# Two banks for the running tile products, and batch 1's normalised rows made by VectorE instead of TensorE transposes

## The chip, the cores and the metric

One Trainium2 chip, one of its cores. The time is the device time of one launch in microseconds. Before the change it is 2794.61 us, the median of three runs (2794.59 to 2795.62). The profiled execution, from which every row below comes, took 2796.74 us, with a span of 2794.9 us from its first to its last instruction and a mean granted TensorE clock of 0.997.

## The reference, cut to what matters

One transformer block with adaptive modulation, on x of shape (2, 2048, 576), with 16 heads of 36 and a hidden width of 2304.

```python
mod = swish(c) @ w_mod + b_mod
sh_msa, sc_msa, g_msa, sh_mlp, sc_mlp, g_mlp = split(mod, 6, axis=1)
xn = _ln(x) * (1 + sc_msa[:, None, :]) + sh_msa[:, None, :]
qkv = xn @ w_qkv + b_qkv
q, k, v = heads of qkv
q = _ln(q, g_q);  k = _ln(k, g_k)
attn = softmax(q k^T * HD ** -0.5)
x = x + g_msa * ((attn v) @ w_proj + b_proj)
xn2 = _ln(x) * (1 + sc_mlp) + sh_mlp
x = x + g_mlp * (gelu(xn2 @ w1 + b1) @ w2 + b2)
```

`_ln` subtracts the mean over the last axis and divides by the root of the variance plus 1e-6, on the 576 features of a row for xn and on the 36 features of a head for q and k.

## The kernel before, in words

Nearly full precision is had from 16-bit matmuls: each factor is cut into a high and a low f16 half, and three products are added. A tile of 128 rows times the 432 columns of one group of heads (q, k and v of four heads) takes 14 matmuls (`split_products`, which `tile_products` issues).

**Order of the work.** After a start (modulation, batch 0's rows normalised, turned and multiplied for the first group of heads) come 8 groups G, one for each batch and four heads: 0 to 3 are batch 0, 4 to 7 are batch 1. A group is 16 units u, a unit is one head and 512 queries, and a unit has 8 steps s. In a step

- TensorE makes two score matmuls (`scores`) and, three steps behind (LAG), four matmuls of probabilities with v (`sums`);
- ScalarE takes the exponential of 128x1024 scores into `p` (line 697);
- VectorE takes the low part `plo` of it (line 890), which `sums` needs.

`scores` of a step needs the exponential of two steps before; the exponential of a step needs `sums` of four steps before; both are semaphore counts with credits given at the start. Every engine executes its own list of instructions in order, and waits where that list says so.

**The tile that runs along.** In each unit one tile of the next group is made. TensorE issues seven of its matmuls in step 0 and seven in step 1, all into one PSUM bank (`tile_bank`), after a wait until VectorE has read the tile before out of it (`t_yn`). ScalarE copies v out in step 2 and squares q and k in step 3, VectorE sums the squares in step 3 (`tile_sum`), GpSimd adds eps and takes the power -0.5 (lines 568 and 570), VectorE scales in step 6 (`tile_normal`, lines 854 and 857), and in the next unit ScalarE writes the high parts in steps 0 and 1 (`tile_high`, `tile_high_again`) and VectorE the low parts in step 1 (`tile_low`, line 863). SyncE then issues one DMA transpose into `qkT` of the next group; the first scores of that group wait for the last of them.

**Batch 1's rows.** They are made beside batch 0's attention. In group 0 VectorE takes their statistics. In group 1 (`Y_IN`) VectorE normalises one tile of 128 rows in each unit (lines 914 and 917) and SyncE stores it to `y_dram`. In group 2 (`HATS_IN`) SyncE loads it back, TensorE turns it with five f32 transposes into `hat_bank` (`hat_turns`, line 1139), ScalarE applies scale and shift while it reads the bank (`hats`, line 669) and makes the high half, and VectorE makes the low half (lines 921 and 922). `tile_products` reads them from group 3's last unit on.

**Weights.** In units 1 to 8 of groups 0 and 1 the weights of the third and fourth heads' groups are centred and cut (`sum_word`, `centre_word`, `high_word`, `low_word`). In groups 4 to 6 ScalarE and VectorE cut one slice of the later weights per unit in step 5 (`word_high`, `word_lower`, lines 679 and 868).

**GpSimd** makes the v operands of the next head once in four units (`head`, lines 549 to 553), in units 2, 6, 10 and 14, after that unit's power.

**Group 7** makes no tiles; instead the projection and the first part of the MLP of the first 512 rows begin there (`rest.tensor_early`, `vector_early`, `gpsimd_early`): GpSimd adds two partial sums in units 1, 3, 4, 5 and 7 (line 1511), VectorE multiplies by the inverse denominators in step 3 of the same units, which it had inverted in step 5 of group 6's last unit (line 1597). After group 7 the MLP is TensorE work almost alone.

Of the kernel before, what the change touches and what calls it, by code (L numbers as in the profile page):

```python
# [17 lines left out]
HD = H // NH  # L18
# [41 lines left out]
class Start:  # L60
# [9 lines left out]
    def __init__(self, nc, ctx, keep, place, ps, wq, xhi, x, c, w_mod, b_mod, w_qkv, b_qkv, g_q, g_k, b2, gates_dram):  # L70
# [20 lines left out]
        later = [sb(f"later{g}", [P, QK, N // 2], F32, at) for g, at in ((2, 126720), (3, 75520))]  # L91
# [10 lines left out]
        self.gates_ready, self.gates_stored = sem("gates_ready"), sem("gates_stored")  # L102
        self.landed = [sem(f"landed{g}") for g in range(self.AHEAD)]
# [193 lines left out]
    def centre_word(self, pool, n, i):  # L297
        m, heads = n * self.SLICED + i, self.word[n][i][:, 0:2 * GW].rearrange("p (e d) -> p e d", d=HD)
        pool.wait_ge(self.w_sum, m + 1)
        pool.tensor_scalar(self.lone_mean[:, :], self.lone[:, :], 1.0 / HD, None, ALU.mult).then_inc(self.w_mean, 1)  # L300
# [42 lines left out]
def attention_mlp(nc, keep, place, x, c, w_mod, b_mod, w_qkv, b_qkv, g_q, g_k, b2, sums_dram, den_dram, rden_dram, y_dram, out, halves,  # L343
# [3 lines left out]
    with ExitStack() as ctx:  # L347
# [4 lines left out]
        STATS_IN, Y_IN, HATS_IN = NG - 4, NG - 3, NG - 2  # L352
        PARTS = ((0, 0, 4, 2, 0), (1, 0, 4, 4, 1), (2, 0, 2, 5, 2), (2, 2, 4, 6, 3), (3, 0, 2, 7, 4), (3, 2, 3, 8, 5), (3, 3, 4, 9, 5))
        RAWS, STORED = 9, (4, 4, 2, 2, 2, 2)
# [36 lines left out]
        hat_bank = ps[:, 6, :]  # L391
        tile_bank, second_bank = ps[:, 7, :], ps[:, 5, :]
# [13 lines left out]
        n_loaded, n_stats, n_mv, n_var, n_rstd, n_y, n_whole, n_stored = (  # L406
            sem("n_" + n) for n in ("loaded", "stats", "mv", "var", "rstd", "y", "whole", "stored"))
# [8 lines left out]
        ny_loaded, n_turned, n_aff, n_hi, n_lo = (sem("n_" + n) for n in ("y_loaded", "turned", "aff", "hi", "lo"))  # L416
# [3 lines left out]
        ends = Ends(t_mm, t_yn, t_stored, scores_ready, head_ready, pv_done, exp_done, oT_ready, oT_stored, n_lo)  # L420
        start = Start(nc, ctx, keep, place, ps, wq, xhi, x, c, w_mod, b_mod, w_qkv, b_qkv, g_q, g_k, b2, gates_dram)
        rest = Mlp(nc, ctx, keep, place, ps, ends, x, sums_dram, den_dram, rden_dram, out, halves, b1, gates_dram)
        block = ctx.enter_context(nc.Block())

        @block.sync
        def _(sp):
# [23 lines left out]
            start.load_tail(sp)  # L450
            start.load_b2(sp, y_ready)
            sp.wait_ge(start.rows_ready, 2)
            turn_heads(0)
# [7 lines left out]
            start.load_words(sp, 0)  # L461
# [15 lines left out]

            def unit(G, u):
# [3 lines left out]
                if G == Y_IN:  # L482
                    if u == 0:
                        sp.wait_ge(n_mv, NT + 1)
                    sp.wait_ge(n_stored, 16 * u + 16)
                    sp.dma_start(xy[:, 0:H], xf[bass.ds(N + u * P, P), :]).then_inc(n_loaded, 16)
                if G == HATS_IN:
                    if u == 0:
                        sp.wait_ge(n_stored, 16 * NT + 16)
                    sp.wait_ge(n_lo, u + 1)  # L490
                    sp.dma_start(xy[:, :], y_dram[bass.ds(u * P, P), :]).then_inc(ny_loaded, 16)
# [12 lines left out]
                if G < GROUPS - 1:  # L504
                    sp.wait_ge(t_low, U + 2)
                    sp.wait_ge(t_high, 2 * U + 3)
                    sp.dma_start_transpose(qkT[(G + 1) % 2][:, :, bass.ds(u * P, P)],
# [31 lines left out]
        def _(pool):  # L539
# [73 lines left out]
            for m in range(1, 5):  # L613
                power(m)
# [1272 lines left out]
```

## Time and profile before

| | us |
|---|---|
| median of the runs | 2794.61 |
| the profiled execution | 2796.74 |
| its span | 2794.9 |
| TensorE busy | 2750.6 |
| VectorE busy | 1988.5 |
| ScalarE busy | 1517.0 |
| GpSimd busy | 669.4 |

Shares of busy time say little here, because three parts follow on each other: the start, to 103.5 us; the eight groups, to 1821.8 us; and the rest. Within the groups the exponential (line 697) that opens each unit is a good clock: from one to the next is a unit.

### The profile page before, as it was taken

Reading aid. Unit: us, or ns where it says so; the run is one execution under the profiler, and the core shown is the slowest. Engines: PE = TensorE matmul, PEld = TensorE weight load, DVE = VectorE, ACT = ScalarE, POOL = GpSimd, SP = SyncE. Lnnn points to the kernel's source line nnn. Section 1 sums busy time; section 2 is a strip of 40 time slices with the busy share of each in tenths; the row PEclk is TensorE's granted clock in tenths of the full one; section 3 lists DMA queues with packets and bytes.
Section 4 is the critical chain, followed back from the end, with each engine's and each line's share of the span. In section 5 each row is a group of like instructions: output and inputs, shape, how many; then the busy total and the mean of one; then the engine's idle time right before and its main releaser. Section 6 shows DMA issues by size and latency. Waiting matters only on the chain.

```text
span 2794.9 us, 42813 instructions
## 1 busy us (share of the span) xinstructions
PE 2750.6 (98%) x14754; PEld 1415.5 (51%) x14754; DVE 1988.5 (71%) x2699; ACT 1517.0 (54%) x2232; POOL 669.4 (24%) x526
## 2 busy tenths in 40 slices
PE   6999999999999999999999999999999999999999
PEld 3444444444444444444444434447566575756656
DVE  7799999888888888888898899953534334353421
ACT  4777777788877777777777777621111112111110
POOL 2553343323233333333343321200000000000000
PEclk9999999999999999999999999999999999999999
DMA  6512322222211122223223243041120202112000
GB/s 222 96 32 66 92 75 79 76 52 48 53 30 32 34 66 67 69 68 74 70 75 78 53 119 112 14 156 53 40 76 16 91 13 79 51 41 76 16 18 18
DMA packets 238609, 181.28 MB, mean 65 GB/s; under 512 B 151511, under 2 KB 187805, under 8 KB 237765
## 3 DMA queue, kind: packets, MB, share of 16 engines
q1 hardware_dynamic: 238182, 179.31, 23.5%
q8 instruction: 96, 1.57, 0.2%
q14 instruction: 43, 0.35, 0.0%
q10 hardware_dynamic: 288, 0.04, 0.0%
HBM read 99.70 MB, written 46.04 MB: 52 GB/s over the span
## 4 chain that ended last, share of the span: by engine, by line
PE 93%; DVE 3%; ACT 1%; issue 1%; SPq 1%; DMA 1%; POOL 1%; ACTq 0%; DVEq 0%
PE at_ps L1760 19%; PE at_ps L1109 15%; PE at_ps L1106 15%; PE at_ps L1097 15%; PE at_ps L1786 15%; PE at_ps L1128 10%; DVE at_plo L890 2%; PE at_ps L1161 1%; PE at_ps L1779 1%; PE at_ps L1724 1%; PE at_ps L1741 1%; ACT at_p L697 0%; DMA st_wm_first<-in_L_cond_b_mod 0%; PE at_ps L210 0%; PE at_ps L1139 0%
## 5 line engine op out<-in xcount | busy, mean ns | idle before, releaser
L890 DVE TENSOR_TENSOR at_plo<-at_p 128x1024 fp32r<-128x1024 f32 x1024 | 1267.9, 1259 | 184.5 <-ACT at_p L697 181.7
L697 ACT ACTIVATE at_p<-at_ps 128x1024 f32<-128x1024 f32 x1024 | 1047.5, 1026 | 407.2 <-PE at_ps L1097 406.4
L1109 PE MATMUL at_ps<-at_plo,at_vr 128*37 128x512 f32 x2048 | 1073.5, 592 | 0.0
L1106 PE MATMUL at_ps<-at_p,at_v 128*73 128x512 bf16 x2048 | 797.2, 389 | 4.9 <-DVE at_plo L890 4.7
L1760 PE MATMUL at_ps<-ml_w2s,ml_hid 128*128 128x288 f16 x3456 | 429.8, 287 | 2.0 <-issue 2.0
L1760 PEld LDWEIGHTS at_ps<-ml_w2s,ml_hid 128*128 128x128 f16 x3456 | 338.7, 98 | 87.9 <-issue 2.5
L1786 PE MATMUL at_ps<-ml_xhi,ml_w 128*128 128x512 f16 x1296 | 381.9, 379 | 0.0
L1106 PEld LDWEIGHTS at_ps<-at_p,at_v 128*73 128x73 f16 x2048 | 232.8, 114 | 249.6 <-DVE at_plo L890 10.5
L568 POOL TENSOR_TENSOR at_tssq<-at_tssq,head_eps 128x8 f32<-128x8 f32 x112 | 123.8, 1106 | 959.8 <-DVE at_tssq L850 959.8
L1109 PEld LDWEIGHTS at_ps<-at_plo,at_vr 128*37 128x37 f32 x2048 | 233.7, 114 | 221.7 <-issue 0.7
L1097 PE MATMUL at_ps<-at_qk_even 109*128 (+1 forms) x1024 | 310.1, 385 | 2.4 <-ACT at_p L697 2.4
L1097 PE MATMUL at_ps<-at_qk_odd 109*128 (+1 forms) x1024 | 309.5, 384 | 0.0
L1128 PE MATMUL at_ps<-at_wq,at_xhi 128*128 128x432 f16 x1008 | 295.8, 348 | 4.3 <-DVE at_txc L854 3.7
L1642 DVE TENSOR_TENSOR ml_part<-at_ps,ml_gates 128x576 f32<-128x576 f32 x64 | 48.5, 757 | 348.1 <-PE at_ps L1760 348.1
L1568 ACT ACTIVATE ml_g<-at_ps,ml_b1col 128x512 f32<-128x512 f32 x144 | 96.2, 686 | 362.6 <-PE at_ps L1779 249.8
L570 POOL TENSOR_TENSOR at_tssq<-at_tssq,power 128x8 f32<-128x8 f32 x112 | 248.3, 2217 | 8.8
L1551 ACT ACTIVATE ml_aff<-at_ps,cols 128x512 f32<-128x512 f32 x40 | 31.0, 776 | 345.8 <-PE at_ps L1724 345.8
L1786 PE MATMUL at_ps<-ml_xlo,ml_w 128*128 128x512 f16 x576 | 218.3, 379 | 0.0
L1688 DVE CAST ml_hid<-ml_g 128x512 f16<-128x512 f32 x144 | 61.2, 425 | 201.8 <-ACT ml_g L1568 201.8
L1786 PEld LDWEIGHTS at_ps<-ml_xhi,ml_w 128*128 128x128 f16 x1296 | 123.5, 98 | 157.6 <-issue 15.7
L1128 PE MATMUL at_ps<-at_wq,at_xlo 128*128 128x432 f16 (+1 forms) x560 | 193.9, 346 | 0.0
L1527 POOL TENSOR_TENSOR ml_rstd<-ml_mv,eps 128x4 f32<-128x4 f32 x7 | 1.4, 202 | 741.8 <-DVE ml_mv L1676 741.8
(182 smaller groups left out, 2280.3 us busy)
## 6 DMA issues: line engine op xcount, KB each, us to landing
head_sums<-at_oT SPq DMA_DIRECT2D x256, 72.0 KB
ml_held<-head_sums SPq DMA_DIRECT2D x64, 256.0 KB
at_xy<-in_L_cond_w SPq DMA_DIRECT2D x34, 288.0 KB
w_halves<-at_wq SPq DMA_DIRECT2D x68, 144.0 KB
at_xy<-in_x SPq DMA_DIRECT2D x32, 288.0 KB, 2.9
ml_x<-in_x SPq DMA_DIRECT2D x8, 1152.0 KB, 5.8
out<-ml_x SPq DMA_DIRECT2D x7, 1152.0 KB, 4.5
ml_held<-head_rden SPq DMA_DIRECT2D x24, 216.0 KB
```

Of the source, the lines that this page charges most:

```text
L568: pool.tensor_tensor(tssq[:, 1, :], tssq[:, 0, :], keep.head_eps[:, 0:QK], ALU.add).then_inc(t_msq, 1)
L570: pool.tensor_tensor(tssq[:, 1, :], tssq[:, 1, :], keep.power[:, 0:QK], ALU.pow).then_inc(t_rstd, 1)
L697: act.activation(p[:, s % NP, :], ps[:, 2 * (s % 2):2 * (s % 2) + 2, :].rearrange("p a n -> p (a n)"), ACT.Exp).then_inc(exp_done, 1)
L890: nc.vector.tensor_tensor(plo[:, s % NP, :], p[:, s % NP, :], high, ALU.subtract).then_inc(plo_ready, 1)
L1097: last = nc.tensor.matmul(ps[:, 2 * (s % 2) + a, :], qk[0:SW, GH + h, (2 * s + a) * P:(2 * s + a + 1) * P], qk[0:SW, h, bass.ds(qc * CH, C ...
L1106: nc.tensor.matmul(acc[0:VW, bass.ds((U % 2) * CH, CH)], v16[:, h % 2, 2 * s + a, 0:VW], high, start=(s == 0 and a == 0), stop=False, skip ...
L1109: last = nc.tensor.matmul(acc[0:RW, bass.ds((U % 2) * CH, CH)], vr[:, h % 2, 2 * s + a, 0:RW], plo[:, s % NP, a * CH:(a + 1) * CH], start= ...
L1128: last = nc.tensor.matmul(bank[:, 0:3 * GW], l, rhs[:, g * 3 * GW:(g + 1) * 3 * GW], start=(n == 0), stop=(n == len(ops) - 1))
L1568: act.activation(self.g32[:, f % 2, :], self.up_bank(f), ACT.Gelu_apprx_tanh, bias=self.b1col[:, f:f + 1], scale=1.0 / WS).then_inc(self.g ...
L1688: nc.vector.tensor_copy(self.hhi[:, f, :], self.g32[:, f % 2, :]).then_inc(self.hhi_ready, 1)
L1760: last = nc.tensor.matmul(self.pair(i)[:, half, :], l, w[:, half * HALF:(half + 1) * HALF], start=(n == 0), stop=(n == len(ops) - 1))
L1786: last = nc.tensor.matmul(self.up_bank(f), w, xs, start=first and n == 0, stop=not first and n == len(ops) - 1)
```

## The change

- **Two banks for tile products.** `tile_bank` becomes a function of the tile's number, banks 6 and 7 in turn. TensorE waits for the reading of the tile before last. VectorE's scaling of a tile (`tile_normal`) moves from step 6 to step 0 of the next unit, `tile_high` to step 1, `tile_high_again` and `tile_low` to step 2, the square and its sum to step 4. Unit 0 has the same order as the others.
- **eps by VectorE.** `tile_sum` is followed by a small VectorE addition; GpSimd's line 568 is gone, its power stays.
- **Batch 1's rows by VectorE.** Group 1's normalising and its store, group 2's load, TensorE's transposes and ScalarE's scaling are gone. In group 2, units 1 to 10, and group 3, units 1 to 6, one tile of 128 rows is handled per unit: SyncE loads x; VectorE in step 5 does `hat_scaled` and then `hat_shifted`, each 128x576; ScalarE in step 6 writes the high half in two copies (`hat_high`); VectorE in step 7 writes the low half (`hat_lower`, 128x576); SyncE issues two DMA transposes into `xhi` and `xlo`, and loads the next tile. Scale and shift are rows, stored to DRAM at the start (`store_mods`) and spread over the partitions by a load at the head of each of the two groups, where GpSimd adds 1 to the scale.
- **Start.** The last four tiles of the first 2048 rows are four parts of their own (before, two together and two alone); GpSimd's first half of `head_of` moves up between two powers; SyncE issues `load_words` behind the first unit's transpose, not ahead of it.
- **Group 7.** The inversion of the denominators moves from unit 15 to unit 14 of group 6, GpSimd's additions wait for the first `sums` of their own unit, and VectorE's multiplications move from step 3 to step 5.

```diff
-        PARTS = (..., (3, 0, 2, 7, 4), (3, 2, 3, 8, 5), (3, 3, 4, 9, 5))
-        RAWS, STORED = 9, (4, 4, 2, 2, 2, 2)
+        HATS = 10
+        SCALED_AT, SHIFTED_AT, HAT_HIGH_AT, HAT_LOW_AT = 5, 5, 6, 7
+        PARTS = (..., (3, 0, 1, 7, 4), (3, 1, 2, 8, 4), (3, 2, 3, 9, 5), (3, 3, 4, 10, 5))
+        RAWS, STORED = 10, (4, 4, 2, 2, 2, 2)
...
-        hat_bank = ps[:, 6, :]
-        tile_bank, second_bank = ps[:, 7, :], ps[:, 5, :]
+        tile_pair = ps[:, 6:8, :].rearrange("p a n -> p (a n)")
+        def tile_bank(X, c0, c1):
+            return tile_pair[:, bass.ds((X % 2) * CH + c0, c1 - c0)]
...
+            def load_hat(r):
+                sp.wait_ge(n_lo, r + 1)
+                sp.dma_start(xy[:, 0:H], xf[N + r * P:N + r * P + P, :]).then_inc(n_loaded, 16)
...
+                if U == 0:
+                    start.load_words(sp, 0)
...
+                if r is not None:
+                    sp.wait_ge(n_lo, r + 2)
+                    if hat_of(G, u + 1) is not None:
+                        load_hat(r + 1)
+                    for part, whole in ((hat_hi, xhi), (hat_lo, xlo)):
+                        sp.dma_start_transpose(whole[:, :, r * P:(r + 1) * P], part[G - HATS_IN]).then_inc(n_turned, 16)
...
             def tile_power(X):
-                pool.wait_ge(t_ssq, X + 1)
-                pool.tensor_tensor(tssq[:, 1, :], tssq[:, 0, :], keep.head_eps[:, 0:QK], ALU.add).then_inc(t_msq, 1)
                 pool.wait_ge(t_msq, X + 1)
...
+                if u == 0 and G in (HATS_IN, HATS_IN + 1):
+                    n = G - HATS_IN
+                    pool.wait_ge(n_rows, 16 * (n + 1))
+                    pool.tensor_scalar(scale_row[n], scale_row[n], 1.0, None, ALU.add)
+                    pool.memset(hat_lo[n][:, H:KC * P], 1.0).then_inc(n_hole, 1)
...
+            def hat_high(n, r):
+                act.wait_ge(n_hat, r + 1)
+                act.wait_ge(n_turned, 32 * r + 32)
+                act.copy(hat_hi[n][:, 0:H], xy[:, 0:H])
+                act.copy(hat_hi[n][:, H:KC * P], xy[:, KF * P:H]).then_inc(n_hi, 1)
...
-                    if tail and s == (1 if first else 0):
+                    if tail and s == 1:
                         tile_high(U)
-                    if tail and s == (2 if first else 1):
+                    if tail and s == 2:
                         tile_high_again()
...
-                    if fresh and s == 3:
-                        tile_square(X, second_bank if first else tile_bank)
-                    if G == HATS_IN and s == 5:
-                        hats(u, range(KF))
-                    if G == HATS_IN and s == 7:
-                        hats(u, (KF,))
-                        hats_high(u)
+                    if fresh and s == 4:
+                        tile_square(X)
+                    if hat is not None and s == HAT_HIGH_AT:
+                        hat_high(G - HATS_IN, hat)
...
             def tile_sum(X):
                 dve.wait_ge(t_sq, X + 1)
                 nc.vector.tensor_reduce(tssq[:, 0, :], txc[:, :, :], AX.X, ALU.add).then_inc(t_ssq, 1)
+                dve.wait_ge(t_ssq, X + 1)
+                nc.vector.tensor_scalar_add(tssq[:, 1, :], tssq[:, 0, :], HD * EPS * WS * WS).then_inc(t_msq, 1)
...
+            def hat_scaled(n, r):
+                dve.wait_ge(n_loaded, 16 * (NT + r + 1))
+                nc.vector.scalar_tensor_tensor(out=halved(xy[:, 0:H]), in0=halved(xy[:, 0:H]), scalar=nmv[:, r, 0:1], in1=scale_row[n],
+                                               op0=ALU.subtract, op1=ALU.mult).then_inc(n_scaled, 1)
+
+            def hat_shifted(n, r):
+                dve.wait_ge(n_scaled, r + 1)
+                nc.vector.scalar_tensor_tensor(out=halved(xy[:, 0:H]), in0=halved(xy[:, 0:H]), scalar=nrstd[:, 1, r:r + 1], in1=shift_row[n],
+                                               op0=ALU.mult, op1=ALU.add).then_inc(n_hat, 1)
+
+            def hat_lower(n, r):
+                dve.wait_ge(n_hi, r + 1)
+                nc.vector.tensor_tensor(hat_lo[n][:, 0:H], xy[:, 0:H], hat_hi[n][:, 0:H], ALU.subtract).then_inc(n_lo, 1)
...
-                    if tail and s == (2 if first else 1):
+                    if tail and s == 0:
+                        tile_normal(U)
+                    if tail and s == 2:
                         tile_low(U)
...
-                    if fresh and s == 3:
+                    if fresh and s == 4:
                         tile_sum(X)
-                    if fresh and s == 6:
-                        tile_normal(X, second_bank if first else tile_bank)
...
-                    if bank is tile_bank:
-                        pe.wait_ge(t_yn, X + 1)
+                    if not isinstance(X, int) or X >= 2:
+                        pe.wait_ge(t_yn, X)
...
-                    if G == HATS_IN and s == 4:
-                        hat_turns(u, range(KF))
-                    if G == HATS_IN and s == 7:
-                        hat_turns(u, (KF,))
...
+            pool.wait_ge(self.ends.pv_done, (self.UNITS_DONE - UNITS + u) * STEPS + 2)
...
-        if u in self.MULTIPLY_IN and s == 3:
+        if u in self.MULTIPLY_IN and s == 5:
```

## Rows read from the trace of the kernel before

**Rows 1.** Windows: groups 2, 3, 4 and 7, and what follows the groups

```profile
core 0: us, PE busy (x) PEld busy (x) DVE busy (x) ACT busy (x) POOL busy (x), PEclk, DMA share, GB/s
...
537.70:767.30 229.60, 226.87 (x1078) 107.17 (x1077) 192.86 (x243) 190.36 (x321) 58.43 (x52) 1.00 0.22 53
767.30:981.80 214.50, 214.50 (x990) 94.66 (x988) 181.03 (x209) 155.55 (x226) 76.51 (x52) 1.00 0.15 33
981.80:1197.20 215.40, 215.40 (x994) 94.97 (x993) 189.84 (x225) 163.33 (x240) 77.34 (x52) 1.00 0.26 66
1626.30:1821.80 195.50, 192.18 (x902) 85.99 (x900) 184.14 (x176) 143.13 (x154) 39.66 (x33) 1.00 0.29 89
1821.80:2794.90 973.10, 967.00 (x6407) 615.96 (x6404) 390.53 (x704) 163.57 (x251) 52.40 (x46) 1.00 0.16 52
```

**Rows 2.** Waits of TensorE in the groups, whole span: sum, times, longest

```profile
PE at_ps L1106 <- DVE at_plo L890: 4.7, 7, 1.2
PE at_ps L1128 <- DVE at_txc L854: 3.7, 9, 0.7
```

**Rows 3.** Groups of instructions, group 2: transposes, and the tile products' wait

```profile
L1128 PE MATMUL at_ps<-at_wq,at_xhi 128*128 128x432 f16 x146 | 42.8, 348 | 2.7 <-DVE at_txc L854 2.2
L1139 PE MATMUL at_ps<-ident,at_xy 128*128 128x128 f32 x80 | 13.9, 272 | 0.0
```

**Rows 4.** Timeline of ScalarE, one unit of group 3: start, duration, instruction

```profile
874.04 1.02 ACT L697 ACTIVATE at_p<-at_ps 128x1024 f32<-128x1024 f32 x1 [0.42 <-PE at_ps L1097]
874.96 0.43 ACT L643 CAST at_tstk<-at_txc 128x288 f16<-128x288 f32 x1
...
880.18 0.28 ACT L651 ACTIVATE at_v<-at_ps 128x144 f32 x1
880.40 0.58 ACT L663 COPY at_oT<-at_ps 73x512 f32 x1
880.88 1.02 ACT L697 ACTIVATE at_p<-at_ps 128x1024 f32<-128x1024 f32 x1
```

**Rows 5.** Timeline of VectorE, the same unit

```profile
881.93 1.23 DVE L890 TENSOR_TENSOR at_plo<-at_p 128x1024 fp32r<-128x1024 f32 x1 [0.39 <-ACT at_p L697]
883.07 0.45 DVE L850 TENSOR_REDUCE at_tssq<-at_txc 128x8 f32<-128x288 f32 x1
883.44 3.58 DVE L890 TENSOR_TENSOR at_plo<-at_p 128x1024 fp32r<-128x1024 f32 x3
887.32 0.46 DVE L854 SCALAR_TENSOR_TENSOR at_txc<-at_ps,at_tssq 128x288 f32<-128x288 f32 x1 [0.30 <-POOL at_tssq L570]
887.81 0.31 DVE L857 TENSOR_TENSOR at_txc<-at_txc,gain 128x144 f32<-128x144 f32 x1
888.04 2.35 DVE L890 TENSOR_TENSOR at_plo<-at_p 128x1024 fp32r<-128x1024 f32 x2
```

**Rows 6.** Timeline of TensorE: scores of step 1, one unit on

```profile
889.47 0.38 PE L1097 MATMUL at_ps<-at_qk_odd 109*128 x1
```

**Rows 7.** Groups of instructions, group 5: operations of 128x576, and the low parts

```profile
L868 DVE SCALAR_TENSOR_TENSOR at_wq<-at_xy,at_wq 128x576 f16<-128x576 f32 x16 | 12.0, 751 | 0.0
L679 ACT ACTIVATE at_wq<-at_xy 128x576 f16<-128x576 f32 x16 | 10.8, 675 | 0.0
L863 DVE TENSOR_TENSOR at_tstk<-at_txc,at_tstk 128x144 f16<-128x144 f32 x32 | 8.4, 304 | 0.0
```

**Rows 8.** Timeline of VectorE around a `head`, group 4

```profile
1023.01 5.00 DVE L890 TENSOR_TENSOR at_plo<-at_p 128x1024 fp32r<-128x1024 f32 x3
```

**Rows 9.** The same stretch on GpSimd: the longest operation of `head`

```profile
1024.70 2.24 POOL L553 TENSOR_TENSOR at_v<-at_v 128x576 f16<-128x576 f32 x1
```

**Rows 10.** Timeline of VectorE, end of group 6

```profile
1625.20 1.74 DVE L1597 RECIPROCAL ml_den<-ml_den 128x256 f32<-128x256 f32 x1
```

**Rows 11.** Timeline of TensorE: first unit

```profile
107.67 0.61 PE L1106 MATMUL at_ps<-at_p,at_v 128*73 128x512 bf16 x1 [1.18 <-DVE at_plo L890]
```

**Rows 12.** Transfers: issuer, number, median us from issue to landing

```profile
at_qk_even<-at_tstk SPq DMA_TRANSPOSE x48, 3.1
```

More of the change, by code:

```diff
@@ L132, in load_tail, with store_mods @@
         sp.dma_start(self.wm_tail[KT:KT + 1, :], self.b_mod[2 * H:6 * H].unsqueeze(0)).then_inc(self.wm_loaded[1][1], 16)
+    def store_mods(self, sp, mods_dram):
+        sp.wait_ge(self.rows_taken, 1)
+        for n, q in ((0, 32), (1, 0)):
+            sp.dma_start(mods_dram[n:n + 1, :], self.rows[0][q + 16:q + 17, 0:H]).then_inc(self.mods_stored, 16)
     def load_b2(self, sp, free):
@@ L405, in attention_mlp @@
             sem("t_" + n) for n in ("mm", "sq", "ssq", "msq", "rstd", "yn", "yg", "high", "low", "stored"))
-        n_loaded, n_stats, n_mv, n_var, n_rstd, n_y, n_whole, n_stored = (
-            sem("n_" + n) for n in ("loaded", "stats", "mv", "var", "rstd", "y", "whole", "stored"))
+        n_loaded, n_stats, n_mv, n_var, n_rstd = (sem("n_" + n) for n in ("loaded", "stats", "mv", "var", "rstd"))
+        n_rows, n_hole, n_scaled, n_hat, n_hi, n_lo, n_turned = (
+            sem("n_" + n) for n in ("rows", "hole", "scaled", "hat", "hi", "lo", "turned"))
         w_loaded, w_high, w_low, w_stored = sem("w_loaded"), sem("w_high"), sem("w_low"), sem("w_stored")
@@ L481, in unit @@
                     load_row(2 * u - UNITS)
[L482 to L491, printed above, removed]
+                r = hat_of(G, u)
+                if G in (HATS_IN, HATS_IN + 1) and u == 0:
+                    sp.wait_ge(scores_ready, G * UNITS * STEPS)
+                    both = start.later[G % 2][:, 2:6, HOLE // 2:HOLE // 2 + HALF]
+                    sp.dma_start(both, bcast(mods_dram.rearrange("v (a n) -> (v a) n", a=2), 0, P)).then_inc(n_rows, 16)
+                    load_hat(hat_of(G, 1))
                 i = U - SLICED * UNITS
@@ L612, in _ @@
                 pool.memset(stk[:, a, :, :, SW:P], 0.0).then_inc(start.stk_ready, 1)
-            for m in range(1, 5):
+            power(1)
+            head_of(0, 0, NT // 2)
+            for m in range(2, len(PARTS)):
                 power(m)
-            power(5)
-            power(6)
             tile_power(0)
-            head_of(0, 0, NT // 2)
             head_of(1, NT // 2, NT)
@@ L809, in _ @@
             square(4)
-            high(2)
             raw(7)
             square(5)
+            high(2)
             raw(8)
@@ L815, in _ @@
             high(3)
+            raw(9)
+            square(7)
             high(4)
+            high(5)
             tile_v(0, NT)
             tile_square(0)
-            high(5)
             high(6)
+            high(7)
             for G in range(GROUPS):
@@ L832, in _ @@
                     with act.Fori(start.SLICED + 2, UNITS - 1) as u:
+                        unit(G, u)
+                elif G in (HATS_IN, HATS_IN + 1):
+                    done, r0 = (HATS, 0) if G == HATS_IN else (NT - HATS, HATS)
+                    unit(G, 0)
+                    with act.Fori(1, done + 1) as u:
+                        unit(G, u, hat=u + r0 - 1)
+                    with act.Fori(done + 1, UNITS - 1) as u:
                         unit(G, u)
@@ L1084, in _ @@
                         unit(G, u, True)
-                    with dve.Fori(sliced, UNITS - 1) as u:
+                    for u in range(sliced, UNITS - 1):
                         unit(G, u)
@@ L1113, in sums, with tile_products @@
                 last.then_inc(pv_done, 1)
-            def tile_products(X, t, G, some, bank=tile_bank):
+            def tile_products(X, t, G, some):
                 ops = list(split_products(xhi, xlo, wq, bass.ds(t * P, P), slice(None)))
@@ L1218, in _ @@
             tile_products(0, 0, 1, range(0, 14))
[L1219 removed]
+            tile_products(1, 1, 1, range(0, 14))
             pe.wait_ge(start.gain_step, 4)
```

131 lines of the change are left out of this document (62 added, 69 removed).

## The prediction

> **What bounds the kernel now.** I read the windows first. In group 4 TensorE is busy for all of 215.4 us, in group 3 for all of 214.5 [rows 1]; a unit is 215.4 / 16 = 13.46 us and nothing but TensorE's own work sets it. VectorE is at 88% and ScalarE at 76% there, so both have room on average. Behind the groups TensorE is busy for 967.0 of 973.1 us, and the change leaves that part alone. Second, the waits: inside the groups TensorE waits 4.7 us for low parts of probabilities and 3.7 us for the bank of the tile products [rows 2]; that is all that better order can win, beside 2.4 us or so at the very start. Third, group 2, where batch 1's rows are turned: 229.6 us, 14.2 over group 4. Of this 2.7 us are waits, 2.2 of them for the bank, and the rest is TensorE's 80 transposes [rows 1, 3]. Last, the timelines of one plain unit on ScalarE, VectorE and TensorE [rows 4 to 6], because the question is whether the new work in 16 units still fits beside TensorE's 13.46 us.
>
> **What is removed.** Groups 2 and 3 together take 229.6 + 214.5 = 444.1 us. With neither transposes nor waits they are 32 units of 13.46, or 430.8: -13.3 us. The second bank also ends the waits for the bank outside group 2: 3.7 - 2.2 = 1.5 us [rows 2, 3], so -1.5; I see no bound of it but 0 and -1.5. Group 1's and group 2's row traffic through DRAM and VectorE's normalising in group 1 are hidden now and their removal gives nothing of its own. GpSimd loses the addition of eps; it has been idle most of the time, so that gives nothing either, and the small operation on VectorE costs some 0.1 us per unit under TensorE's work.
>
> **What is added, and whether it is hidden.** Three VectorE operations of 128x576 each: the one of that size that the trace has takes 0.751 us [rows 7], and the next VectorE instruction starts about 0.08 us ahead of a record's end (3.58 us for three low parts that start 1.14 apart [rows 5]). So 0.75 + 0.03 (the first waits for itself, as 854 and 857 show [rows 5]) + 0.67 + 0.67 = 2.1 us. A unit's VectorE work then is 8 low parts x 1.14 = 9.1, scaling 0.72 (887.32 to 888.04), tile low parts 0.44 (twice 0.22, their 0.304 less 0.08 [rows 7]), sum and eps 0.36 + 0.2, and 2.1: 13.0 us. That is under 13.46, so on the sum of work alone it fits. But these operations are strung on one chain with ScalarE's, and each engine is in order. I walk along it, with S the start of `hat_scaled` in step 5:
>
> - `hat_shifted` starts at S + 0.78 and its record ends at S + 1.53. VectorE goes on with the low part of step 6. ScalarE has been waiting at `hat_high` since it finished step 6's exponential. Its two copies take about 0.58 (0.675 less the overlap [rows 7]) and 0.12, so step 7's exponential starts at S + 2.3 and VectorE has it at S + 3.34 (a record of 1.02 and 0.04 until VectorE sees it).
> - VectorE: low part of step 7 to S + 4.48, `hat_lower` to 5.15, low part of step 0 to 6.29, then the tile's scaling, whose second operation is done at 7.12 (0.49 + 0.31 + 0.03 [rows 5]).
> - ScalarE waits for that in step 1 (`tile_high`), which takes 0.34 (0.43 less the overlap [rows 4]), so step 2's exponential starts at S + 7.46; its low part starts at 8.52.
> - ScalarE after it: 0.92 for the exponential (874.04 to 874.96), three copies of 144 columns of 0.2 each, 0.48 for the output copy (880.40 to 880.88) [rows 4]. Step 3's exponential starts at S + 9.5, its low part at 10.55.
> - VectorE: two low parts 2.28, sum and eps 0.58, low part of step 5 1.14. The next S is at S + 14.55.
>
> So the chain takes 14.5 us to come round, of which VectorE idles 1.5, against TensorE's 13.46: 1.1 us more per unit. TensorE does feel it. Its scores of step 1 need step 7's exponential, at S + 3.38. In the first such unit S is the low part of step 3, two more, the sum and eps, and one more: 881.93 + 1.14 + 1.14 + 0.58 + 1.14 = 885.93 on the plain unit's clock [rows 5], and the exponential is there at 889.31; the scores started at 889.47 [rows 6]. The first unit costs nothing and all slack is used up. Each later one adds 1.1: 9 x 1.1 - 0.1 = 9.8 in group 2 and 5 x 1.1 - 0.1 = 5.4 in group 3, together 15.2. What errs here is the sum of some fifteen durations; with 0.3 either way per unit (the low parts' gaps and the waits are what I know least) the 14 units give 11.0 to 19.4.
>
> On top comes `head` on GpSimd. When it runs, three low parts take 5.00 us where they take 3.58 otherwise, 1.4 us more [rows 5, 8]. In plain units TensorE covers that. In the new ones the chain is what counts; it has about 0.7 us of VectorE idle before step 7's low part and 0.4 twice later, so I take 0.9 of the 1.4. Units 2, 6, 10 of group 2 and 2, 6 of group 3 have a `head`, the one in unit 10 half outside: 4 x 0.9 = 3.6, bounds 0 and 5 x 1.4 = 7.
>
> The row of `head` shows it: its longest operation takes 2.24 us [rows 9] while the low parts beside it stretch by 1.4 in all. The Trainium skill, "SBUF — State Buffer", section "Who interferes with whom", says that a VectorE instruction with two SBUF inputs contends with a GpSimd instruction that reads SBUF, and that the one issued second blocks fully. All three new operations have two such inputs. The trace agrees in kind; by that rule each of them could lose a whole GpSimd operation, and what that would make is the second rival.
>
> New waits with no price as far as I see: the load of the next tile and the two DMA transposes are issued behind `hat_lower` (S + 5.2) and are wanted by S + 14.5 and S + 16.1; a transpose lands in 3.1 us [rows 12]. SyncE's queue has the unit's other transpose and the stores of sums between them, issued at about S + 10, and has room. At the end of a group the last tile's low part is now in step 2, at about 882.4 on the plain unit's clock, and with 3.1 us lands at 885.6, a good 1 us ahead of the next group's first scores, some 2.7 before 889.47 [rows 6, 12]. If it lands later, each of seven group boundaries pays.
>
> **Start and group 7.** In the first unit TensorE waits 1.18 us for the first low part [rows 11], which stood behind the tile's scaling on VectorE and now is ahead of it: -1.2, bounds 0 and -2.4. The start's four single tiles are more instructions for the same work, and GpSimd's powers are its chain; I count nothing. For group 7, 4.7 - 1.2 = 3.5 us of waits for low parts lie around it [rows 2, 11]. The inversion of 1.74 us [rows 10] stands between low parts where TensorE has no tile products to cover it; in unit 14 it has them, less the `head` there. GpSimd's second addition no longer follows directly on a `head`. The fifth unit's load of both a multiplication and a low part stays. I take half: -1.7, bounds 0 and -3.5.
>
> **The sum.** -13.3 - 1.5 + 15.2 + 3.6 - 1.2 - 1.7 = +1.1 us. The profiled execution took 2796.74, 2.1 more than the median of the runs, so this is 2797.8 for such an execution and 2795.7 for the median. A difference of 0.2%, 5.6 us, is about what can be told from none.
>
> **The rivals.** (1) *The chain does not bind.* VectorE's 13.0 us of work do fit, and if the exponentials catch up (ScalarE finds its operands ready, as it does in group 4) the new units stay at 13.46. Then 15.2 and 3.6 go: 2795.7 - 18.8 = 2777. For it speaks that group 1, with normalising on VectorE, runs without such a loss; against it, that group 1 had nothing for ScalarE to wait on between steps 6 and 7. A half-binding chain, 0.5 us a unit, gives 2777 + 7 + 1 = 2785. (2) *GpSimd's `head` blocks VectorE more than it did.* With more VectorE instructions of two inputs, each `head` costs its whole longest operation and more; at 2.24 each, five make 11.2 for my 3.6: 2795.7 + 7.6 = 2803, slower by 0.3%. It decides from 1.6 us a `head`, where the sum passes +5.6. For it speaks that the chain has no cover; against it, the rows of plain units, 1.4. (3) *A transpose lands late at the group boundaries*, in place of the wait for the bank: 7 x 1 us at most, 2802. (4) *The second bank gives nothing*, since VectorE's lateness only moves from the bank to the low parts: 1.5 less won, 2797, inside the first case.
>
> **How the numbers follow.** The forecast, a chain of 14.2 to 14.85 us, has 0.60, with its own range 2789 to 2802 (the 14 units' ends, and the other bounds taken half-way); of this 0.42 is within 0.2%, 0.08 faster, 0.10 slower. Rival 1 with its half-way case has 0.26, faster. Rivals 2 and 3 have 0.14, slower by over 0.2% nearly all. So faster 0.34, same 0.43, slower 0.23. The range has to take in rival 1's far end, 2777, with 2 us below it for its other terms' bounds (group 7 and the start could give 1.8 and 1.2 more), and go up to 2804.
>
> **What would show it.** Right: units of group 2 from the second to the tenth at 14.3 to 14.8 us and those behind them at 13.46; ScalarE's wait for `hat_shifted` of 2.5 us or so in each; TensorE's waits in these units at the scores, for exponentials, and hardly at the low parts; no wait of TensorE for the tile's scaling anywhere; no transposes by TensorE. Wrong: units at 13.5 there (rival 1), or TensorE waiting with low parts late after each `head` (rival 2), or scores waiting for a transfer in a group's first step (rival 3). The forecast fails first if one of the durations on the chain is not on it, for instance if the high copies start while the second operation still runs.

## The result and the profile after

The kernel after takes 2803.9 us, the median of eight runs (2801.55 to 2805.68); the kernel before takes 2795.1 beside it. The ratio is 1.0034, with a 95% interval of 1.0026 to 1.0043: slower by 0.3%. The forecast was 2795.7 and "no difference". The profiled execution took 2805.68 us with a span of 2803.6, 8.7 us over the span of before (2794.9). The forecast's range reached to 2804, which just takes the result in. That is luck: by the chain and its bounds alone it ended at 2802, and the rest was for costlier `head`s and late transfers.

The windows of the kernel after, group 2, 3, 4, 6, 7 and what follows:

```profile
core 0: us, PE busy (x) PEld busy (x) DVE busy (x) ACT busy (x) POOL busy (x), PEclk, DMA share, GB/s
532.82:764.81 231.99, 219.77 (x994) 94.00 (x992) 202.39 (x255) 157.46 (x244) 63.46 (x39) 1.00 0.27 58
764.81:990.39 225.58, 218.21 (x994) 94.44 (x993) 192.50 (x244) 155.68 (x237) 64.01 (x39) 1.00 0.24 50
990.39:1205.84 215.45, 215.45 (x994) 95.03 (x993) 188.44 (x240) 161.96 (x240) 65.40 (x37) 1.00 0.26 66
1421.29:1636.39 215.10, 213.47 (x980) 93.40 (x978) 188.38 (x236) 159.43 (x235) 64.06 (x36) 1.00 0.27 67
1636.39:1830.51 194.12, 191.80 (x902) 86.27 (x900) 181.71 (x175) 143.15 (x154) 43.89 (x33) 1.00 0.29 89
1830.51:2803.60 973.09, 966.95 (x6406) 615.96 (x6404) 389.86 (x704) 163.61 (x251) 52.48 (x46) 1.00 0.16 52
```

Against [rows 1], groups 2 and 3 take 457.6 us, not 444.1; group 4, group 7 (1.4 less) and the rest are as before. The 1078 matmuls of group 2 are 994: the transposes are gone, and the group is longer all the same. The other differences are small: the groups begin at 100.59 us (before 103.47), groups 0 and 1 are 0.5 and 1.5 shorter, group 6 is 1.5 longer. Together -2.9 - 0.5 - 1.5 + 13.5 + 1.5 - 1.4 = +8.7. From one exponential that opens a unit to the next, group 2 reads 13.57, 15.65, 14.77, 16.07, three of 14.77, 16.06, three of 14.77, and from there 13.46; group 3 is alike with six units. A unit with a row takes 14.77, one in which a `head` still runs 1.3 more.

TensorE's waits in the kernel after, whole span:

```profile
PE at_ps L1151 <- ACT at_p L730: 24.4, 42, 2.6
PE at_ps L1160 <- DVE at_plo L950: 2.7, 6, 0.9
```

The wait for the tile's scaling [rows 2] is gone from the list, and the scores (line 1151 now) wait for exponentials. TensorE, the second unit with a row (its first exponential is at 562.04): the scores of step 5, then those of the next step 1:

```profile
569.43 0.60 PE L1151 MATMUL at_ps<-at_qk_even 109*128 x2 [0.37 <-ACT at_p L730]
...
576.00 0.35 PE L1182 MATMUL at_ps<-at_wq,at_xhi 128*128 128x432 f16 x1
576.96 0.61 PE L1151 MATMUL at_ps<-at_qk_even 109*128 x2 [0.61 <-ACT at_p L730]
```

A stall is longer than its bracket. The records of two product matmuls that follow on each other start 0.18 apart and last 0.35, so the last one reaches some 0.17 into the stall: 0.37 + 0.61 + 2 x 0.17 = 1.3, the whole of 14.77 - 13.46. That is also why group 2's windows show 219.8 us of busy TensorE where group 4 shows 215.4 for the same 994 matmuls: 23 stalls of 0.17 are 3.9 of the 4.3. Lengths of units count here, busy time doesn't.

VectorE once round the chain, from the S of the first row to that of the second (line 926 is `hat_scaled`, 931 `hat_shifted`, 936 `hat_lower`, 950 the low part, 896 and 899 the tile's scaling):

```profile
558.61 0.81 DVE L926 SCALAR_TENSOR_TENSOR at_xy<-at_xy,at_nmv,st_later 128x576 f32<-128x576 f32 x1
559.45 0.82 DVE L931 SCALAR_TENSOR_TENSOR at_xy<-at_xy,at_nrstd,st_later 128x576 f32<-128x576 f32 x1
560.19 1.22 DVE L950 TENSOR_TENSOR at_plo<-at_p 128x1024 fp32r<-128x1024 f32 x1
562.17 1.23 DVE L950 TENSOR_TENSOR at_plo<-at_p 128x1024 fp32r<-128x1024 f32 x1 [0.76 <-ACT at_p L730]
563.31 0.75 DVE L936 TENSOR_TENSOR at_qk_odd<-at_xy,at_qk_odd 128x576 f16<-128x576 f32 x1
563.98 1.22 DVE L950 TENSOR_TENSOR at_plo<-at_p 128x1024 fp32r<-128x1024 f32 x1
565.11 0.45 DVE L896 SCALAR_TENSOR_TENSOR at_txc<-at_ps,at_tssq 128x288 f32<-128x288 f32 x1
565.60 0.31 DVE L899 TENSOR_TENSOR at_txc<-at_txc,gain 128x144 f32<-128x144 f32 x1
...
573.38 0.81 DVE L926 SCALAR_TENSOR_TENSOR at_xy<-at_xy,at_nmv,st_later 128x576 f32<-128x576 f32 x1
```

and ScalarE beside it, with two copies of the step 2 before:

```profile
552.51 0.30 ACT L684 CAST at_tstk<-at_txc 128x144 f16<-128x144 f32 x1
552.71 0.33 ACT L685 CAST at_tstk<-at_txc 128x144 f16<-128x144 f32 x1
...
560.39 0.67 ACT L706 CAST at_qk_odd<-at_xy 128x576 f16<-128x576 f32 x1 [2.33 <-DVE at_xy L931]
560.97 0.24 ACT L707 CAST at_qk_odd<-at_xy 128x64 f16<-128x64 f32 x1
561.12 2.85 ACT L730 ACTIVATE at_p<-at_ps 128x1024 f32<-128x1024 f32 x3
566.02 0.43 ACT L681 CAST at_tstk<-at_txc 128x288 f16<-128x288 f32 x1 [2.06 <-DVE at_txc L899]
```

The chain of the forecast is there link by link: ScalarE idles 2.33 us for `hat_shifted`, then, three exponentials later, 2.06 for the tile's scaling, and VectorE idles in between for the exponential that ScalarE had to hold back. From S = 558.61 to the next S = 573.38 is 14.77 where 14.55 was forecast. In the next round a `head` runs; VectorE, and GpSimd beside it:

```profile
576.94 1.47 DVE L950 TENSOR_TENSOR at_plo<-at_p 128x1024 fp32r<-128x1024 f32 x1 [0.75 <-ACT at_p L730]
578.33 0.75 DVE L936 TENSOR_TENSOR at_qk_odd<-at_xy,at_qk_odd 128x576 f16<-128x576 f32 x1
579.00 2.27 DVE L950 TENSOR_TENSOR at_plo<-at_p 128x1024 fp32r<-128x1024 f32 x1
...
589.45 0.81 DVE L926 SCALAR_TENSOR_TENSOR at_xy<-at_xy,at_nmv,st_later 128x576 f32<-128x576 f32 x1
```

```profile
576.67 0.67 POOL L586 CAST at_v<-at_v 128x576 f16<-128x576 f32 x1
...
578.42 1.77 POOL L589 TENSOR_TENSOR at_v<-at_v 128x576 f16<-128x576 f32 x1
```

Two low parts stretch, from 1.22 to 1.47 and 2.27, together by 1.30, and from this S to the next is 16.07, 1.30 over the others: all of it goes onto the chain. Neither `hat_` operation is hit here.

### The profile page after: what moved, and what is told of

It is laid out like the page before. It is cut to its first block, busy times and chain, and to the rows that moved or that the text cites. A ratio compares the mean times of both kernels' runs of the same rounds, so it can differ in the third digit from the quotient of the medians.

```text
span 2803.6 us, 42286 instructions
## 1 busy us (share of the span) xinstructions
PE 2744.9 (98%) x14674; PEld 1402.1 (50%) x14674; DVE 1994.4 (71%) x2800; ACT 1475.9 (53%) x2174; POOL 615.9 (22%) x420
## 4 chain that ended last, share of the span: by engine, by line
PE 86%; DVE 7%; ACT 3%; issue 1%; SPq 1%; DMA 1%; POOL 0%; ACTq 0%; DVEq 0%
PE at_ps L1801 19%; PE at_ps L1827 15%; PE at_ps L1163 14%; PE at_ps L1160 14%; PE at_ps L1151 14%; PE at_ps L1182 9%; DVE at_plo L950 5%; ACT at_p L730 1%; PE at_ps L1820 1%; PE at_ps L1765 1%; PE at_ps L1782 1%; PE at_ps L1206 0%; DVE at_xy L931 0%; ACT at_oT L701 0%; DVE at_xy L926 0%
## 5 line engine op out<-in xcount | busy, mean ns | idle before, releaser
L950 DVE TENSOR_TENSOR at_plo<-at_p 128x1024 fp32r<-128x1024 f32 x1024 | 1245.0, 1246 | 194.6 <-ACT at_p L730 191.4
L730 ACT ACTIVATE at_p<-at_ps 128x1024 f32<-128x1024 f32 x1024 | 1034.2, 1028 | 365.9 <-PE at_ps L1151 364.9
L604 POOL TENSOR_TENSOR at_tssq<-at_tssq,power 128x8 f32<-128x8 f32 x112 | 277.3, 2475 | 1039.1 <-DVE at_tssq L892 1039.1
L1151 PEld LDWEIGHTS at_ps<-at_qk_even 109*128 109x128 f16 x1024 | 68.8, 99 | 177.0 <-issue 125.0
```

The costliest lines, as they stand in the source:

```text
L604: pool.tensor_tensor(tssq[:, 1, :], tssq[:, 1, :], keep.power[:, 0:QK], ALU.pow).then_inc(t_rstd, 1)
L730: act.activation(p[:, s % NP, :], ps[:, 2 * (s % 2):2 * (s % 2) + 2, :].rearrange("p a n -> p (a n)"), ACT.Exp).then_inc(exp_done, 1)
L950: nc.vector.tensor_tensor(plo[:, s % NP, :], p[:, s % NP, :], high, ALU.subtract).then_inc(plo_ready, 1)
L1151: last = nc.tensor.matmul(ps[:, 2 * (s % 2) + a, :], qk[0:SW, GH + h, (2 * s + a) * P:(2 * s + a + 1) * P], qk[0:SW, h, bass.ds(qc * CH, C ...
```

## The experiments

The main theory: what the new rows cost is the chain between VectorE and ScalarE, with `head` on top. "G2+G3" is groups 2 and 3 together, 457.6 in the kernel after; spans and unit lengths are of the profiled execution, times are medians.

**No rows.** Nothing of batch 1's rows is done; batch 1's tiles are made from batch 0's rows, and the rest stays.

```diff
-            if G == HATS_IN and 1 <= u <= HATS: ...
+            return None
```

> Leaves out batch 1's normalised rows altogether (VectorE's three operations, ScalarE's two copies, GpSimd's two, the loads and transposes of the 16 units), so batch 1's tiles are made from batch 0's rows. All theories agree that the 16 units fall back to 13.46 us and groups 2 and 3 to 430.8 from 457.6, a span of 2776.8 for 2803.6. It sizes what everything else in the change brings: if the second bank, the start and group 7 brought nothing, the span would be 2794.9 - 13.3 = 2781.6; by the units of the changed kernel they bring 4 to 5 us. Rival 'late transfers or the bank still cost': units of groups 2 and 3 stay above 13.5 without the rows.

Measured: span 2776.9 (one run, 2778.99). The units of groups 2 and 3 are 13.46 (the first of each 13.57), G2+G3 is 431.0. So the row work costs 457.6 - 431.0 = 26.6 us, and taking the transposes and their waits out of the kernel before had given 444.1 - 431.0 = 13.1.

**High copies one step later,** in step 7.

```diff
-        SCALED_AT, SHIFTED_AT, HAT_HIGH_AT, HAT_LOW_AT = 5, 5, 6, 7
+        SCALED_AT, SHIFTED_AT, HAT_HIGH_AT, HAT_LOW_AT = 5, 5, 7, 7
```

> ScalarE makes the high half in step 7, after that step's exponential, not in step 6. The same work on each engine. Theory 'ring': the exponential of step 7 no longer waits for VectorE's two long operations, but the tile's scaling still stands behind the lower half, so the ring is 1.58 + 4 VectorE operations (1.14, 1.14, 0.67, 1.14) + 0.83 + 0.34 to step 2's exponential, and 7.02 from there to the next long operation (as measured in the changed kernel): 13.9 us per unit for 14.77; groups 2 and 3 together at 440 to 444 us for 457.6, the whole about 2788 to 2790. Rival 'work': VectorE simply has too much to do, the order does not matter: units stay at 14.7 or more and the time at 2804. Rival 'head': the 16.06 us units stay 1.3 above the others under both.

Measured: 2792.3 us, ratio to before 0.9995 (0.9985 to 1.0004); G2+G3 445.0; units with a row 13.91, behind a `head` 15.43. No instruction was taken away and the units lost 0.86 us, so it is not VectorE's sum of work that sets them. ScalarE:

```profile
560.73 0.67 ACT L706 CAST at_qk_odd<-at_xy 128x576 f16<-128x576 f32 x1 [0.96 <-DVE at_xy L931]
```

One exponential that stood behind this wait now stands ahead of it.

**Also the low part in the next unit's step 1.**

```diff
-        SCALED_AT, SHIFTED_AT, HAT_HIGH_AT, HAT_LOW_AT = 5, 5, 7, 7
+        SCALED_AT, SHIFTED_AT, HAT_HIGH_AT, HAT_LOW_AT = 5, 5, 7, 1
-                    if hat is not None and s == HAT_LOW_AT:
-                        hat_lower(G - HATS_IN, hat)
+                    if isinstance(u, int) and u and hat_of(G, u - 1) is not None and s == HAT_LOW_AT:
+                        hat_lower(G - HATS_IN, hat_of(G, u - 1))
```

> As e2, and the low half of the row moves from step 7 to step 1 of the next unit, behind the tile's scaling. Theory 'ring': 0.67 us less on it, 13.2 us, which is under TensorE's 13.46: the 16 units at 13.5, groups 2 and 3 together at 432 to 437, the whole at 2779 to 2784, faster than both kernels. The units behind a head lose up to 1 us each. Rival 'work': still 14.7 a unit, 2804. Rival 'head': units behind a head at 14.8, 2785 or more.

Measured: 2783.7 us, 0.9963 (0.9950 to 0.9977); G2+G3 436.3, plain row units 13.25 to 13.46, behind a `head` 14.91, the first 14.73. (The first unit's excess is only the lead that the exponentials had over TensorE: TensorE stalls nowhere in group 2 but behind the three `head`s.)

**The second long operation twice** (batch 1's rows are other numbers by it).

```diff
+                for again, done in ((0, n_scaled), (1, n_hat)):
```

> The second long operation is done twice (scale and shift applied once more, so batch 1's rows are other numbers). Theory 'ring': each repetition adds its whole 0.84 us to every one of the 16 units, 15.6 us for 14.77, and 13 us to the span, 2817. Rival 'slack': if VectorE's idle 1.4 us per unit could take it, the units stay at 14.8 and the span at 2804.

Measured: span 2815.1 (one run, 2817.19); G2+G3 470.9, 13.3 more for 16 more operations. The pair takes its place on the chain in full:

```profile
558.52 0.81 DVE L926 SCALAR_TENSOR_TENSOR at_xy<-at_xy,at_nmv,st_later 128x576 f32<-128x576 f32 x1
559.37 1.67 DVE L932 SCALAR_TENSOR_TENSOR at_xy<-at_xy,at_nrstd,st_later 128x576 f32<-128x576 f32 x2
560.96 1.22 DVE L951 TENSOR_TENSOR at_plo<-at_p 128x1024 fp32r<-128x1024 f32 x1
```

**A thin `head`:** in groups 2 and 3 it handles one of the 36 columns, with all its instructions.

```diff
+                w = 1 if 9 <= Hh <= 16 else HD
```

> The changed kernel, but GpSimd's head in groups 2 and 3 handles one column in 36 (v's operands of eight heads are wrong, the instructions and waits stay). Theory 'head': the five units at 16.06 us go to 14.77 like the others, 6.5 us off groups 2 and 3 (457.6 to 451.1), a span of about 2797. Rival: the 1.3 us come from something else in every fourth unit; they stay and so does the span, 2803.6 less what the start varies by, 2 us.

Measured: span 2793.1 (one run, 2795.19); G2+G3 451.03; every row unit but the first is 14.77, those behind a `head` too. Five `head`s cost 6.5 us on the chain, 1.3 each: three show as units of 16.06, and the last of each group as the unit behind the last row, 13.48 and 13.49 before and 12.21 and 12.23 here. Groups 2 and 3:

```profile
530.56:758.64 228.08, 218.77 (x994) 94.34 (x992) 198.53 (x256) 157.37 (x245) 50.88 (x39) 1.00 0.29 60
758.64:981.59 222.95, 217.58 (x994) 94.67 (x993) 189.87 (x244) 155.55 (x237) 51.74 (x39) 1.00 0.24 51
```

**The tile's steps as before,** two banks and rows kept: scaling in step 6, high parts in 0 and 1, low in 1, square and sum in 3.

```diff
-                    if tail and s == 0:
-                        tile_normal(U)
+                    if fresh and s == 6:
+                        tile_normal(X)
```

> The changed kernel with the rows by VectorE and both banks, but the running tile in the steps of before: scaling in step 6, high parts in steps 0 and 1, low parts in 1, square and sum in 3. Theory 'ring': what closes it is the tile's scaling in step 0, which ScalarE waits for in step 1; with the scaling in step 6, behind step 6's low part, it is done by the time step 7's exponential is, and what is left is VectorE's work, 13.1 us: units of 13.5, groups 2 and 3 at 431 to 438, the whole at 2778 to 2786. Rival 'rows': the long operations and ScalarE's wait for them in step 6 cost the time by themselves, wherever the tile stands: units of 14 or more, 2795 or more.

Measured: 2779.1 us, 0.9946 (0.9930 to 0.9961); G2+G3 435.4, row units 13.47 and 13.89, those behind a `head` 14.2 and the first 15.24. The steps of the tile moved back together; that the scaling in step 0 was the link is told by ScalarE's waits. Those for it, whole span, in the kernel after and here; the one for `hat_shifted` remains (26.6 and 21.9 us in group 2):

```profile
ACT at_tstk L681 <- DVE at_txc L899: 61.0, 46, 3.4
```

```profile
ACT at_tstk L681 <- DVE at_txc L899: 8.6, 22, 1.8
```

**Low part in the next unit, inversion in unit 13.** The third experiment with `INVERT_IN` 13 in place of 14.

> e3 with the inversion of the denominators in unit 13 of group 6, where no head runs, for unit 14. Theory: in unit 14 the 1.7 us of it and the head make the tile's scaling late and ScalarE waits for it in unit 15, which takes 13.1 us for the 11.7 of the kernel before; it goes to 11.5 or less. 1.5 to 2 us off e3: a span of 2782.5 for 2784.5. Rival: unit 15 is long because the last tile's steps stand there; no change.

Measured: 2779.6 us, 0.9945 (0.9931 to 0.9959). Group 6 takes 213.35 against 215.02 in the third experiment. In unit 14 the inversion shares the unit with `head`, and the last tile's scaling comes late behind both; so what the change won at group 7 (1.4) it lost at the end of group 6 (1.5).

**Rows kept out of units with a `head`:** the kernel of the last paragraph with rows in units 1, 2, 4, 5, 6, 8, 9 and 10 of both groups.

> e7 with the 16 rows in units 1, 2, 4, 5, 6, 8, 9 and 10 of both groups, so that no unit behind a head has a row. Theory 'head': each of the five heads costs 1.1 us in e3 because the unit behind it has a row too; without it TensorE's work covers it. Groups 2 and 3 at 431 to 433 for 436.3, the span at 2777 to 2779. Rival: a head behind a unit with a row is enough to cost 1 us; then e8 is as e7.

Measured: 2781.9 us, 0.9952 (0.9939 to 0.9966), G2+G3 437.1 against 436.4. The theory fell: `head` runs behind the power of its unit and so into the next, and a `head` behind a row unit still costs 1.0 (6.1 us over 431.0 for six of them; 1.1 each for five before), wherever the next row stands. TensorE's only stalls in group 2 are in the units behind a `head`, 3, 7 and 11, at two scores each; in unit 3:

```profile
579.56 0.60 PE L1148 MATMUL at_ps<-at_qk_even 109*128 x2 [0.18 <-ACT at_p L729]
581.55 0.61 PE L1148 MATMUL at_ps<-at_qk_even 109*128 x2 [0.48 <-ACT at_p L729]
```

These, with 0.17 for each record, make the 1.0. (The exponentials read 14.72 in units 1, 4 and 8, where they lose lead and TensorE doesn't stall.)

**The three together:** tile's steps as before, high copies in step 7, inversion in unit 13.

> e6 with the high half in step 7, as in e2, and the inversion in unit 13, as in e7. Theory 'ring': in e6 ScalarE still waits 1.9 to 2.7 us for the second long operation ahead of step 7's exponential, which fits in plain order but leaves nothing for the first unit and a head (13.9 and 14.2 us); taking it off gives groups 2 and 3 together 432 to 434 for 435.4, group 6 some 0.8 less, the span about 2773 to 2774 for 2775.9. Rival: with the tile scaled in step 6 VectorE's work alone is the limit and the place of the high half is worth nothing.

Measured: 2775.4 us (five runs, 2774.17 to 2778.37), 0.9933 (0.9920 to 0.9947): the fastest version, 19 us under before. Its groups 2, 3, 4 and 6:

```profile
530.41:746.86 216.45, 216.00 (x994) 94.80 (x992) 201.81 (x255) 162.38 (x244) 61.11 (x38) 1.00 0.29 62
746.86:963.06 216.20, 215.90 (x994) 94.91 (x993) 193.34 (x244) 159.34 (x237) 62.03 (x38) 1.00 0.25 52
963.06:1178.51 215.45, 215.45 (x994) 95.02 (x993) 191.87 (x239) 163.69 (x241) 64.76 (x36) 1.00 0.26 66
1393.96:1607.21 213.25, 213.22 (x980) 93.50 (x978) 190.80 (x236) 161.34 (x235) 61.59 (x35) 1.00 0.27 67
```

VectorE does as much in group 2 as in the kernel after (201.8 against 202.4 us), and the row work costs 432.6 - 431.0 = 1.6 us in place of 26.6.

**One bank's wait.** The sixth experiment with the wait of before; the bank is still chosen by the tile's number.

```diff
-                        pe.wait_ge(t_yn, X)
+                        pe.wait_ge(t_yn, X + 1)
```

> e6, but TensorE waits until the tile before has been scaled before it makes the next, as it must with one bank (the banks themselves stay two). It prices the second bank where rows are made: the scaling is seen some 0.9 us after the tile products could start, so the 16 units take 14.1 to 14.4 us and groups 2 and 3 8 to 12 us more than e6's 435.4, a span of 2784 to 2788; in plain units 0.1 or nothing. Rival: the scaling is early enough with rows too, no change from 2775.9.

Measured: span 2819.2 (one run, 2821.29), far outside what I expected. G2+G3 is 459.2 against 435.4, and each group with plain tiles and weight slices is 219.0 against 215.45: plain units are 13.77, 0.31 longer, and every fourth is not. VectorE's scaling and TensorE there:

```profile
1039.70 0.44 DVE L896 SCALAR_TENSOR_TENSOR at_txc<-at_ps,at_tssq 128x288 f32<-128x288 f32 x1
1039.73 0.59 PE L1164 MATMUL at_ps<-at_plo,at_vr 128*37 128x512 f32 x1
1040.48 0.54 PE L1183 MATMUL at_ps<-at_wq,at_xhi 128*128 128x432 f16 x2 [0.15 <-issue]
```

Part of the idle time is put down to "issue", in which TensorE's sequencer waits for nothing that the profile shows.

**One fixed bank.** The fastest version with a bank that is a constant, and the same wait.

```diff
-            return tile_pair[:, bass.ds((X % 2) * CH + c0, c1 - c0)]
+            b = X if isinstance(X, int) and X < 2 else 0
+            return tile_pair[:, b * CH + c0:b * CH + c1]
```

> The best version so far (tile steps of before, high copies in step 7, inversion in unit 13; 2775.4 us) with one PSUM bank for the running tile products in place of two, the bank a constant and not chosen by a register. In the run before, where the bank stayed register-addressed and only the wait was that of one bank, every plain unit with tile products lost 0.3 us, of which the profile puts 0.15 down to issue, and groups 2 and 3 went up by 23.8. Theory A: the loss in plain units is the address worked out behind the wait, so with a fixed bank plain groups are back at 215.4 (group 1) while in groups 2 and 3, where the scaling stands behind the rows' operations, TensorE now waits for it in each unit with a row: 14 units at 0.5 to 1.3 more, 440 to 451 for groups 2 and 3 in place of 432.6, and 2783 to 2794 us in all. Theory B (the forecast's term): the bank's waits are worth 1.5 to 4 us in all, 2777 to 2780. Theory C: the 0.3 is the wait itself; then group 1 stays at 218.

Measured: 2810.7 us, 1.0060 (1.0043 to 1.0076); the profiled span is 2806.9, 32.5 over the fastest version's. G2+G3 is 454.4 (+21.7), groups 0 and 1 +3.7 and +1.9, groups 4 and 5 +2.3 each, group 6 +3.1. The medians are 35.3 apart. In groups 2 and 3 A, which expected up to 451, was right in kind and 3 us short. In the plain groups it was wrong and C the nearer one: group 1 is 217.35 where A said 215.4 and C 218, and the plain units read 13.63 to 13.67, so about 0.2 of the 0.31 stays. The rest was the address behind the wait. The same two instructions with the fixed bank, 0.16 us from the end of the scaling's record to the first product where it was 0.34:

```profile
1030.47 0.44 DVE L897 SCALAR_TENSOR_TENSOR at_txc<-at_ps,at_tssq 128x288 f32<-128x288 f32 x1
1031.08 0.54 PE L1184 MATMUL at_ps<-at_wq,at_xhi 128*128 128x432 f16 x2
```

B falls. TensorE in the whole span:

```profile
PE at_ps L1184 <- DVE at_txc L897: 21.6, 23, 1.9
```

A reading of the 0.2, argued and not tried: the added eps operation on VectorE. From the tile's sum to the end of the scaling's record it is 1049.56 - 1044.66 = 4.90 us in the kernel before, and here, in the same unit with the same low parts and weight slice between them, it is 1044.56 - 1039.45 = 5.11. The two lines of this version, and VectorE's eps between:

```profile
1039.45 0.45 DVE L891 TENSOR_REDUCE at_tssq<-at_txc 128x8 f32<-128x288 f32 x1
1039.93 0.17 DVE L893 TENSOR_SCALAR at_tssq<-at_tssq 128x8 f32<-128x8 f32 x1
1040.03 2.37 DVE L951 TENSOR_TENSOR at_plo<-at_p 128x1024 fp32r<-128x1024 f32 x2
```

## Why the prediction was wrong

**The step that failed is the sum of "What is added, and whether it is hidden".** It put the new rows at 15.2 + 3.6 = 18.8 us; the kernel with and without them differs by 26.6. The mechanism stands: the chain of VectorE and ScalarE binds though VectorE's work fits, TensorE waits at the scores for exponentials, and the units behind the rows are back at 13.46. Three terms were mis-sized, all to the same side:

- *A unit of the chain,* 14.55 forecast and 14.77 measured, 1.31 over 13.46 in place of 1.1: 14 x 0.2 = 2.9 us. The long operations last 0.81 and 0.82, not the 0.751 of the nearest row [rows 7]; `hat_high` starts 0.12 behind the second one's record, and step 7's exponential stands at S + 2.51, not 2.3. By the scaling it is 0.08 more: `tile_high`'s exponential is at S + 7.75, not 7.46.
- *The first unit with a row,* -0.1 forecast and +0.9 measured, two of them: 2.0 us. (Group 2 is 16.5 over group 4; less 9 x 1.31 and 3 x 1.3, 0.9 is left. The 15.65 that the exponentials read for it is more, since they had run ahead of TensorE and lose that lead there.) The forecast took the first S from the plain unit of before, 885.93 - 874.04 = 11.89 behind the unit's exponential; it came at 558.61 - 546.39 = 12.22. In step 2 ScalarE now makes two copies that stood in step 1 before, ahead of step 3's exponential (552.51 and 552.71 above). That one starts 7.18 behind the unit's first, before 880.88 - 874.04 = 6.84. The walk counted them in the later units and not in the first. This 0.33 and the 0.21 of the first term are more than the 0.16 of slack: TensorE waited at step 1 (0.24 at 562.19) and, where the forecast looked for nothing, again at step 5, for step 3's exponential behind the tile's scaling (0.37 at 569.43).
- *`head`,* 0.9 each for four and 1.3 each for five: 6.5 less 3.6 is 2.9 us. The forecast let VectorE's idle time on the chain take up part of the stretch. It can't: VectorE idles there because it waits for ScalarE, which waits for VectorE; in a closed chain whatever any member loses is lost.

2.9 + 2.0 + 2.9 = 7.8, and 18.8 + 7.8 = 26.6. The unit's 14.77 lies inside the forecast's own 14.2 to 14.85; the chain's 20.1 is beyond the upper bound (19.4) by the first units, and the `head`s' 6.5 is just inside theirs (7).

**Right or nearly:** what is removed, -13.3 forecast, -13.1 measured. No wait for the scaling, no late transpose at a boundary: TensorE waits for no transfer in the groups, and the first unit of groups 2 to 6 is 13.5 to 13.6, without rows too. The start and groups 0 and 1 gave 4.9 in this execution, against 2.7 forecast for start and bank. The first unit's wait for a low part (1.18 [rows 11]) is gone, but runs with the same start begin their groups between 100.6 and 104.0, so how much of the 1.2 came is not shown. *Group 7 and the inversion* were to give 1.7 and gave nothing: -1.4 in group 7 and +1.5 in group 6, which unit 13 for the inversion gives back.

**The rivals.** (1) The chain doesn't bind: not in this kernel; but the fastest version is that case, 2775.4 where the rival said 2777. (2) `head` blocks VectorE: it was to decide from 1.6 each and is 1.3; the sum reached its side of the bound only with the other two terms. By the Trainium skill, "SBUF — State Buffer", section "Who interferes with whom", of a VectorE instruction with two SBUF inputs and a GpSimd one that reads SBUF, the one issued second is blocked fully. The rows come near it for the subtraction: the low part was issued at 579.00 while GpSimd's 1.77 us operation ran to 580.19, which would cost it 1.19, and it lost 2.27 - 1.22 = 1.05. For the cast they fall short: issued at 576.94 beside an operation that ran to 577.34, the low part would lose 0.40 and lost 0.25. (3) No transfer was late. (4) *The second bank gives nothing:* undecided for the kernel before, where it could give 1.5 at most outside group 2; once the rows are VectorE's and eps too, taking it away costs 32.5 us of span. A price from the waits of the kernel before can hold for a kernel without the rest of the change only.

## What to carry to other kernels

Adding up an engine's work says whether it fits; whether it binds is told by walking the closed chain through both engines, and what has to be counted there are the waits at which an in-order engine holds back work that others need. Such a chain is cheaply cut: the same instructions one step later on ScalarE, and the scaling back in step 6, took 26.6 us to 1.6. When a walk ends near zero, small errors on a chain don't cancel: idle time inside it covers nothing, and an interference is charged in full.

## What the runs showed of the hardware

- A `scalar_tensor_tensor` of 128x576 with both tensors and the result f32 in SBUF and a scalar per partition lasts 0.81 to 0.82 us on VectorE, and 16 more of them made groups 2 and 3 13.3 us longer, 0.83 each; the one with an f16 result took 0.75 [rows 7].
- A PSUM bank chosen by a register, behind a wait that ends last, showed 0.15 us of "issue" ahead of the first matmul, which started 0.34 us behind the record that it waited for, and 0.16 with a fixed bank; plain units were 0.31 longer with it and about 0.2 with a fixed bank.
- GpSimd's operations of 128x576 stretched the low parts beside them by 0.25 (a cast) and 1.05 us (a subtraction), 1.30 for a whole `head`, and removing their width removed all of it.
